# Two heads at a time in the banded attention of an eight-core transformer layer

## The reference, cut to what matters

```python
# x: (16, 2048, 2048) f32
xn = layernorm(x)                                    # no scale, no bias
q, k, v = xn @ Wq, xn @ Wk, xn @ Wv                  # 16 heads of 128
scores = q @ k.T * 128**-0.5 + mask                  # mask: blocks of 64, |bi - bj| <= 2
s = (softmax(scores) @ v) @ Wo
g = silu(xn @ gate_w.T * gate_s) * (xn @ up_w.T * up_s)    # inner size 5632
g = silu((g @ down_w.T) * down_s)
out = x + s * g
```

## Time and profile before

| | us |
|---|---|
| runs timed | 8243.56 and 8642.45, median 8443.0 |
| profiled execution | 8144.83 |
| its span on the slowest core (core 4) | 8143.0 |
| spans of the eight cores | 8102.9 to 8143.0 |
| PE busy / DVE busy / ACT busy | 6012.6 / 1499.4 / 979.5 |
| DMA engines, mean | 104 GB/s |

### The profile page before, as it was taken

How to read it: one execution, slowest core, us unless ns; L and a number is a source line. 1 busy time by engine, 2 the same in 40 slices (tenths; PEclk the granted TensorE clock), 3 DMA queues, 4 the chain that set the end, 5 groups by cost and what they waited for, 6 DMA issues and landing times.

```text
span 8143.0 us, 79584 instructions; the slowest of 8 cores (8102.9 to 8143.0 us)
## 1 busy us (share of the span) xinstructions
PE 6012.6 (74%) x28544; PEld 2761.0 (34%) x28544; DVE 1499.4 (18%) x3939; ACT 979.5 (12%) x2082; POOL 198.4 (2%) x376
## 2 busy tenths in 40 slices
PE   0075231377686776775889988899888998989988
PEld 0032110133332333333334433344333443334433
DVE  0233010122311223223111111111111111111111
ACT  0012010122300222223000000010000010001000
POOL 0000000000000000000000000000000000000000
PEclk9987665688788887887999999999999999999999
DMA  9826969746625435101232234422344223432233
GB/s 123 187 86 119 110 78 111 124 119 155 160 105 136 104 92 131 49 19 57 101 106 75 73 114 127 101 73 83 110 128 104 73 74 114 129 98 83 73 113 126
DMA packets 1121025, 843.13 MB, mean 104 GB/s; under 512 B 570112, under 2 KB 1037056, under 8 KB 1108224
## 3 DMA queue, kind: packets, MB, share of 16 engines
q1 hardware_dynamic: 1076288, 565.39, 26.8%
q0 software_dynamic: 44352, 272.65, 16.8%
HBM read 668.02 MB, written 272.63 MB: 116 GB/s over the span
## 4 chain that ended last, share of the span: by engine, by line
PE 69%; DMA 9%; another core or an unknown queue 6%; DVE 5%; issue 5%; ACT 3%; SPq 3%; DVEq 0%; ACTq 0%; POOLq 0%
PE pp L675 30%; PE pp L387 11%; PE pp L737 7%; PE pp L745 6%; PE pp L414 6%; PE pp L623 5%; DMA arbf<-dwt 3%; PE pp L563 3%; ACT arf L519 3%; DVE arbf L556 2%; SPq L466 1%; SPq L644 1%; DMA wqb<-wq 1%; DMA wkb<-wk 1%
## 5 line engine op out<-in xcount | busy, mean ns | idle before, releaser
L675 PE MATMUL pp<-arbf 128*128 128x512 bf16 x11264 | 2441.2, 380 | 117.1 <-DMA arbf<-gwt 83.6
L387 PE MATMUL pp<-arbf 128*128 128x512 bf16 x4096 | 960.3, 394 | 964.6 <-DMA arbf<-wkb 895.9
L675 PEld LDWEIGHTS pp<-arbf 128*128 128x128 bf16 x11264 | 1103.6, 98 | 1454.6 <-issue 131.4
L387 PEld LDWEIGHTS pp<-arbf 128*128 128x128 bf16 x4096 | 410.0, 101 | 1470.2 <-issue 1043.5
L737 PE MATMUL pp<-arbf 128*128 128x512 bf16 x3072 | 714.1, 391 | 152.4 <-DMA arbf<-dwt 152.4
L563 PE MATMUL pp<-arbf 128*128 128x128 bf16 x1472 | 211.3, 267 | 775.5 <-DVE arbf L556 775.5
L699 DVE SCALAR_TENSOR_TENSOR arbf<-pp,us_sb,arf 128x512 bf16<-128x512 f32 x352 | 264.4, 751 | 2287.1 <-PE pp L675 2287.1
L519 ACT ACTIVATE arf<-pp,b_t 128x384 f32<-128x384 f32 (+1 forms) x512 | 289.4, 565 | 2646.2 <-DVE pp L516 2646.0
L745 PE MATMUL pp<-arbf 128*128 128x512 bf16 x2560 | 573.1, 379 | 31.2 <-DMA arf<-x 7.3
L692 ACT ACTIVATE arf<-pp,gs_sb 128x512 f32<-128x512 f32 x352 | 241.9, 687 | 2261.0 <-PE pp L675 2261.0
L737 PEld LDWEIGHTS pp<-arbf 128*128 128x128 bf16 x3072 | 306.3, 100 | 541.9 <-issue 200.4
(11 more groups left out here) (40 smaller groups left out, 1748.6 us busy)
## 6 DMA issues: line engine op xcount, KB each, us to landing
arbf<-gwt SPq DMA_DIRECT2D x352, 256.0 KB, 4.0
arbf<-uwt SPq DMA_DIRECT2D x352, 256.0 KB, 4.0
arbf<-dwt SPq DMA_DIRECT2D x176, 512.0 KB, 6.3
arf<-x SPq DMA_DIRECT2D x32, 1024.0 KB, 7.8
s_h<-arf POOLq DMA_DIRECT2D x32, 1024.0 KB, 4.2
arf<-s_h SPq DMA_DIRECT2D x128, 256.0 KB, 3.0
arf<-x SPq DMA_DIRECT2D x128, 256.0 KB, 3.3
out<-arf POOLq DMA_DIRECT2D x128, 256.0 KB, 2.5
```

What stands on the lines that cost most here:

```text
L387: i = e.matmul(pb[:], bf(wsl + 128 * hc, 128), bf(XNT + 2048 * hc + 512 * tc, 512), start=(hc == 0), stop=(hc == 15))
L675: i = e.matmul(pb[:], bf(dstoff + 256 * hc + 128 * sub, 128), bf(XNW + 1024 * hc + 512 * tc, 512), start=(hc == 0), stop=(hc == 15))
```

## The change

The loop over 16 heads becomes a loop over 8 pairs. In each step of the loop both heads do their stage B, one after the other, and then both do their stage A. The lag from stage A to stage B falls from four steps to two, so there are 18 steps in place of 20, and three filler items a step in place of two. The reciprocal and the scaling move from the end of stage A to the start of stage B. The output of Exp is bf16 in place of f32. Both heads of the next pair are projected in the fillers of one pair, so the projections of head 1 join those of head 0 ahead of the first pair. `QTS` and `KTS` have four slots in place of two. To make room in SBUF, `XT` and `XNB` have one slot in place of two (both names of the pair point to the same place), and the vector `ds` is loaded ahead of stage 3 into the f32 scratch in place of a tile of its own at the start. Of the background queue, ten or eleven items now go with a pair where it was six or seven with a head.

```diff
-QTS = (49152, 51200)
-KTS = (53248, 55296)
+QTS = (49152, 51200, 53248, 55296)
+KTS = (57344, 59392, 61440, 63488)
-XNB = (68608, 70656)
+XNB = (76800, 76800)
-XT = (0, 2048)
+XT = (0, 0)
...
             for o in proj_ops(0, seq):
                 o()
+            for o in proj_ops(1, seq):
+                o()
-            for head in range(16):
+            for hp in range(8):
+                heads = (2 * hp, 2 * hp + 1)
+                grp = hp // 2
+                if hp % 2 == 0:
+                    prim_v = vproj_ops(grp)
...
+                if hp % 2 == 1 and hp < 7:
+                    base_f += wv_load_ops(grp + 1)
+                if hp < 7:
+                    base_f += proj_ops(heads[0] + 2, seq)
+                    base_f += proj_ops(heads[1] + 2, seq)
                 else:
                     base_f += wo_load_ops(seq)
...
-                def stageA(qb):
+                def stageA(head, qb):
...
+                    em('S', lambda e, pb=pb, W=W, eb=eb, sc4=sc4:
+                        e.activation(
+                            bf(eb, W), pb[:, 0:W], AF.Exp, scale=SCALE,
+                            bias=b12_t[:, 0:1],
+                            accum_out=sums[:, sc4:sc4 + 1]),
-                    em('V', lambda e, qb=qb: e.reciprocal(
-                    em('S', lambda e, W=W, eb=eb, att=att, qb=qb:
-                        e.activation(bf(att, W), f32(eb, W), AF.Copy,
...
-                def stageB(qb):
+                def stageB(head, qb):
+                    sl = head % 2
+                    att = ATT[2 * sl + qb % 2]
+                    attt = ATTT[sl]
+                    ptb, ptk = PT[sl]
                     pa, pak = next_bank()
+                    em('V', lambda e, sc4=sc4: e.reciprocal(
+                        inv[:, sc4:sc4 + 1], sums[:, sc4:sc4 + 1]),
+                    em('S', lambda e, W=W, eb=eb, att=att, sc4=sc4:
+                        e.activation(bf(att, W), bf(eb, W), AF.Copy,
+                                     scale=inv[:, sc4:sc4 + 1]),
...
-                for j in range(20):
+                for j in range(18):
                     vfill(2)
-                    if j >= 4:
-                        stageB(j - 4)
+                    if j >= 2:
+                        stageB(heads[0], j - 2)
+                        stageB(heads[1], j - 2)
                     if j < 16:
-                        stageA(j)
-                    fill(2)
+                        stageA(heads[0], j)
+                        stageA(heads[1], j)
+                    fill(3)
...
+        em('QS', lambda e: e.dma_start(out=f32(DSO, 2048), in_=ds),
+           writes=[(RF, DSO, DSO + 2048)], dma=True)
         for w in range(NW):
             p3_window(w)
```

More of the change, by code:

```diff
@@ L120 @@
 WVS = 40960
-QTS = (49152, 51200)
-KTS = (53248, 55296)
[L123 to L127, removed]
-XNB = (68608, 70656)
-TRBA = 72704
-TRBB = 75520
+QTS = (49152, 51200, 53248, 55296)
+KTS = (57344, 59392, 61440, 63488)
+WQS = 65536
+WKS = 67584
+ATT = (69632, 70144, 70656, 71168)
+ATTT = (71680, 72192)
+OST = (72704, 74752)
+XNB = (76800, 76800)
+TRBA = 78848
+TRBB = 81664
+EB = (84480, 84992, 85504, 86016)
 AOT = 32768
@@ L137 @@
 DWS = 45056
-ARBF_N = 78336
-XT = (0, 2048)
-EB = (4096, 4608)
-SS = (5120, 7168)
+ARBF_N = 86528
+XT = (0, 0)
+SS = (2048, 4096)
+DSO = 6144
 SIL = (0, 512)
@@ L374, in proj_ops @@
         def proj_ops(head, seq):
-            par = head % 2
+            par = head % 4
             ops = []
@@ L479, in p2_seq @@
                 o()
-            for head in range(16):
[L482 to L488, removed]
+            for o in proj_ops(1, seq):
[5 more added lines that the diff above has]
+                    prim_v = vproj_ops(grp)
                 else:
                     prim_v = []
[L491 to L494, removed]
+                base_f = []
+                if hp % 2 == 1 and hp < 7:
[3 more added lines that the diff above has]
+                    base_f += proj_ops(heads[1] + 2, seq)
                 else:
@@ L502, in p2_seq @@
                 fillers.extend(second * 2)
-                def stageA(qb):
+                def stageA(head, qb):
+                    par4 = head % 4
+                    sl = head % 2
+                    qts, kts = QTS[par4], KTS[par4]
                     t0, t1, corners = band(qb)
@@ L517, in stageA @@
                             writes=[(pk, 0, 1)])
[L518 to L522, removed]
-                        reads=[(pk, 0, 1), ('b12', 0, 1)],
-                        writes=[(RF, eb, eb + W), ('sums', qb % 2, qb % 2 + 1)])
-                    em('V', lambda e, qb=qb: e.reciprocal(
[L526 to L530, removed]
-                    em('S', lambda e, W=W, eb=eb, att=att, qb=qb:
-                        e.activation(bf(att, W), f32(eb, W), AF.Copy,
[L533 to L536, removed]
-                def stageB(qb):
+                    sc4 = 2 * sl + qb % 2
+                    eb = EB[sc4]
+                    em('S', lambda e, pb=pb, W=W, eb=eb, sc4=sc4:
[3 more added lines that the diff above has]
+                            accum_out=sums[:, sc4:sc4 + 1]),
+                        reads=[(pk, 0, 1), ('b12', 0, 1)],
+                        writes=[(RB, eb, eb + W), ('sums', sc4, sc4 + 1)])
+                def stageB(head, qb):
+                    sl = head % 2
+                    hh = head % 4
+                    ost = OST[sl]
                     t0, t1, _ = band(qb)
@@ L541, in stageB @@
                     nchunk = W // 128
-                    att = ATT[qb % 4]
-                    attt = ATTT[qb % 2]
-                    ptb, ptk = PT[qb % 2]
-                    pa, pak = next_bank()
+                    sc4 = 2 * sl + qb % 2
+                    eb = EB[sc4]
+                    att = ATT[2 * sl + qb % 2]
+                    attt = ATTT[sl]
+                    ptb, ptk = PT[sl]
+                    pa, pak = next_bank()
+                    em('V', lambda e, sc4=sc4: e.reciprocal(
+                        inv[:, sc4:sc4 + 1], sums[:, sc4:sc4 + 1]),
+                        reads=[('sums', sc4, sc4 + 1)],
+                        writes=[('inv', sc4, sc4 + 1)])
+                    em('S', lambda e, W=W, eb=eb, att=att, sc4=sc4:
+                        e.activation(bf(att, W), bf(eb, W), AF.Copy,
+                                     scale=inv[:, sc4:sc4 + 1]),
+                        reads=[(RB, eb, eb + W), ('inv', sc4, sc4 + 1)],
+                        writes=[(RB, att, att + W)])
                     def tmm(e, nchunk=nchunk, att=att, ptb=ptb):
@@ L591, in vfill @@
                         n -= 1
-                for j in range(20):
+                for j in range(18):
                     vfill(2)
-                    if j >= 4:
-                        stageB(j - 4)
+                    if j >= 2:
+                        stageB(heads[0], j - 2)
+                        stageB(heads[1], j - 2)
                     if j < 16:
-                        stageA(j)
-                    fill(2)
+                        stageA(heads[0], j)
+                        stageA(heads[1], j)
+                    fill(3)
                 vfill(16)
                 fill(len(fillers))
[L602 to L606, removed]
+                for sl in range(2):
+                    em('QG', lambda e, seq=seq, head=heads[sl], ost=OST[sl]:
+                        e.dma_start(out=ao_h[seq, head], in_=bf(ost, 2048)),
+                        reads=[(RB, OST[sl], OST[sl] + 2048)],
+                        writes=[('ao', 16 * seq + heads[sl],
+                                 16 * seq + heads[sl] + 1)], dma=True)
             for k in range(4):
@@ L759, in p3_window @@
                         e.tensor_tensor(f32(osl, 512), pb[:],
-                                        ds_sb[:, c0:c0 + 512], op=ALU.mult),
-                        reads=[(pk, 0, 1), ('ds', 0, 1)],
+                                        f32(DSO + c0, 512), op=ALU.mult),
+                        reads=[(pk, 0, 1), (RF, DSO + c0, DSO + c0 + 512)],
                         writes=[(RF, osl, osl + 512)])
```

12 lines of the change are left out of this document (5 added, 7 removed).

## The result

| | before | changed |
|---|---|---|
| median of all timed runs, us | 8705.12 (10 runs) | 9444.0 (11 runs) |
| lowest run, us | 8131.43 | 8789.3 |
| ratio, undisturbed runs | | 1.074, 95% interval 1.0565 to 1.0914 |
| span of core 4, us | 8143.0 | 8788.5 |

The change makes the kernel 7 to 8% slower. The changed kernel's undisturbed runs took 8789 to 8796 us, and the ratio goes by those; against before's lowest run, 8131 us, it would be 1.081.

A forecast was written before the change was run, and what follows sets the result against it. PE was taken to be bound by its clock and its waits for slices and the DVE copy; 775 + 90 + 14 - 56 = +823 us on 8144.8 gave 8968, forecast as 9020 us, range 8700 to 9380.

The forecast's parts named there:

- the last one, from the profile to the median: Whole kernel: timed runs lie above the profile, so the sum of 8968 us becomes a forecast of 9020 us.
- heads of sequence 1 without the stalls: Sequence 1's attention: +387 us for slower heads and +14 us for three layer-norm tiles standing together.
- Stage B's chain: Attention steps: both heads' links run one after another, 3.04 us per stage B, 7.7 us per step without filler.
- The clock: Projection and V bursts in attention: TensorE's clock falls in the gaps before them, costing 1.7 us a burst.
- The rival in which it holds: Attention gaps: their PE work keeps the clock up, 194 us less and shorter gaps, 8780 us; chance 0.13.
- bf16 out of Exp: Scaling on ACT in attention: reading bf16 takes the same 0.61 us as f32; lower bound 128 us less.
- Single slots: Layer norm, stage 1: x loads only after the previous tile, 12.5 us a tile, +90 us before the first matmul.
- Conversions: Sequence 1: slice loads starve until a conversion run ends; stalls of 242 and 195 us, together 437, -56 us.
- head 1 fills nothing: Rival, attention: head 1's work fills head 0's wait, step under 5.6 us, about 7805 us; chance 0.03.
- no stall vanished: Rival, sequence 1: pair 2's slices land in a pause of POOL's queue, 242 us go, 8780 us; chance 0.09.
- none was added: Rival, SP's queue: the second head's slices come late, another stall of 150 us, 9170 us; chance 0.09.
- the slower heads did not hide: Rival, first sequence: its 387 us hide behind the conversions, about 8580 us; chance 0.04.

The follow-up runs named there:

- a_warm: Changed kernel plus matmuls of no use in PE's gaps, five ahead of each block's transposes and two ahead of its product; 8564 us.
- a_pipe: Changed kernel with both heads' stages B woven link by link, and each block scaled one step after its Exp, one before its transposes; 7784 us.
- a_pipe3: Changed kernel, stages B woven, scaling a step before transposes, two layer-norm slots, conversions spread, four useless matmuls ahead of head 0's product each step; 7565 and 7582 us.
- b_spread: Kernel before with only the background queue reordered: one conversion of up or down weights after every second transposing load of gate weights; 8099 us.

## Why the prediction was right or wrong

The direction and the mechanism held, and the number did not: 9020 was forecast, the range ended at 9380, the median was 9444. Two steps were off, in opposite directions: the sum was 178 us too high, and the step from the profile to the median 603 us too small.

**The step that failed is the last one, from the profile to the median.** The prediction took the offset of a timed run to its profile from two runs of before (99 and 498 us), put half the lower one, 52 us, on the sum and allowed 300 at the range's end. The changed kernel's median lies 655 us above the 8788.5 of core 4. Ten runs of before reach from 8131 to 9124, and its undisturbed runs beside the experiments took 8109 to 8156 us, on either side of the profile's 8145 and not 99 above it. So the offset was no constant to be added: it goes by the share of disturbed runs, and with eight such runs of eleven the median is one of them. What sets that share no run shows. Against undisturbed runs the forecast errs the other way: 9020 and the sum of 8968 stand beside 8789 to 8796, and the sum's ratio of 1.101 (8968 to 8145) lies beyond the end of the measured interval, 1.0914. That 9444 is only 64 us beyond the range is luck: with the sum right, the range would have ended near 9200 (estimate, 9380 - 178).

**The sum, term by term** (core 4 of both):

| term | forecast | measured | how |
|---|---|---|---|
| heads of sequence 2 | +387 | +315 | 1294 to 1609 us, last store at 4504.0 |
| stalls for slices | -56 | -57 | 492.5 to 435.6 us |
| heads of sequence 1 without the stalls | +401 | +312 | 1858 to 2113 us, less the stalls |
| ahead of the first matmul | +90 | +61 | 403.4 to 464.3 us |
| all the rest | 0 | +14 | |
| sum | +823 | +645 | |

*Stage B's chain:* the mechanism was right, and this is the term of the sum that was mis-sized, +627 us (315 and 312) for the +775 of two sequences. One stage B is 2.88 and not 3.04 us, mostly because the reciprocal starts 0.21 us behind the start of the output copy and not 0.32. Two Exps hold ACT for 0.56 us each and not 0.68, since the next starts while the sum is still being read. A step is 7.28 for 7.7, a gap 6.0 for 6.7. With 55 steps and 57 gaps a sequence that is 23 + 40 of the 72 us of sequence 2.

*The clock:* right in kind, a little high in size: 1.5 us a burst in the plain pair above for the 1.7 taken, which is some 11 more of the 72 us (estimate, 57 x 0.2). The rival in which it holds was refuted twice, by the window at 0.76 and by a_warm. The Trainium skill (TensorE: Matmul & The Clock Gate, "HAM oscillation"), by which short bursts can each start cold, agrees with the burst of 9.32 us above. "About 0.7" for the clock was low; it is 0.76.

*bf16 out of Exp:* nothing saved, 0.61 us as taken.

*Single slots:* the lone load of x was taken as 7.5 us; DVE waits 6.2 for it. That makes 61 us of 90.

*Conversions:* the best hit, and it rests on one reading, that a load issued during a run lands when the run ends. (A conversion of the gate, up or down weights writes 2.8 MB in bf16 and reads twice that in f32; the description of the kernel before, 2.8 MB read and half written, is wrong in this.) In the changed kernel too the queues share packet by packet, between 1060 and 1160 us:

```profile
q0 software_dynamic: 539, 10.70, 97.8%
q1 hardware_dynamic: 538, 0.13, 1.0%
```

The Trainium skill (DMA: Bandwidth & Descriptors, "Queues, rings and completion order") has each engine take turns between the queues by packet. The trace agrees, 539 to 538, and shows what follows: the queue with the small packets gets a hundredth of the time.

*Rivals:* the changed kernel's step is 7.28 us and not under 5.6, so head 1 fills nothing; no stall vanished and none was added; the slower heads did not hide. That "faster" was possible by the same idea of pairing is shown by a_pipe, which needed the links woven and the scaling moved a step ahead.

## What to carry to other kernels

Two independent chains do not overlap because both are in a step: on engines that take their lists in order they overlap only if they are emitted link by link, and an instruction that was done steps ahead becomes a link of the chain when it is moved back to its use. Read from the trace which links stand between two uses of the engine that bounds the stage, and count what a burst loses when the clock has fallen in the gap before it. Large conversions in DRAM starve small loads for as long as the run lasts (here 128 KB beside 2.8 MB), so look for where the run's queue stops, not at how big the load is.

## What the runs showed of the hardware that I had not expected

- Matmuls of no use bought time: 3584 more of them, and 8564 us in place of 8789, as the granted clock in the heads went from 0.76 to 1.00. In the short gaps of a_pipe3 four more a step took the clock from 0.92 to 0.98 and made the attention 47 us longer.
- Exp with a row sum takes 0.58 us and its read of the sum 0.19, but the next Exp starts 0.57 us after it: 3194.74, 3195.31, then the scaling at 3195.86.
- The same program's cores differ by 157 us (7857 and 8015 us on cores 0 and 1, both at 0.97 in stage 3) in b_spread, where the conversions come in short runs; their slice stalls differ by 154 us. Those of before lie within 40 us.
